# Attention with latent heads and a LoRA layer on one core: the next group's keys and values are projected one to two windows earlier

## The reference

```
q  = rope(x @ w_q);  k = rope(x @ w_k);  v = x @ w_v          # k, v: 8 sets, each used by 4 heads
lk = rope((x @ w_lq) @ w_lk);  lv = x @ w_lv                  # 32 latent heads
out = causal_attn(q, k, v) @ w_o + causal_attn(q, lk, lv) @ w_lo
```

## Time and profile before

| | |
|---|---|
| median of 3 runs | 2101.74 us (2096.83 to 2101.92) |
| the profiled execution's own time | 2100.59 us |
| its span (first to last instruction) | 2098.8 us |
| PE busy | 2037.8 us, 97% |
| DVE, ACT, POOL busy | 1490.7, 1203.1, 893.1 us |
| mean granted PE clock | 0.995 of full speed |

### The profile page before, as it was taken

The page is one execution under the profiler, slowest core; times in us unless marked ns, Lnnn a source line. Parts: engine busy times, 40 slices in busy tenths (PEclk is TensorE's granted clock), DMA queues, the critical chain, the costliest instruction groups (busy, mean ns, idle before and its releaser), DMA issues.

```text
span 2098.8 us, 33401 instructions
## 1 busy us (share of the span) xinstructions
PE 2037.8 (97%) x11724; PEld 1767.5 (84%) x11724; DVE 1490.7 (71%) x2878; ACT 1203.1 (57%) x2503; POOL 893.1 (43%) x687
## 2 busy tenths in 40 slices
PE   6999999999999999999999999999999999999988
PEld 5888888888888888888888888888888888888777
DVE  6677777776776777777777767777677777777765
ACT  3665656666565655566566565666656565556541
POOL 4344444434543454444534444443454345444311
PEclk9999999999999999999999999999999999999999
DMA  3111111111011111211111121111111111111121
GB/s 103 42 38 36 48 28 36 37 42 47 25 44 36 34 42 36 42 31 43 32 43 37 37 48 30 34 37 43 47 26 43 38 32 42 36 43 32 32 51 41
DMA packets 101941, 83.78 MB, mean 40 GB/s; under 512 B 28296, under 2 KB 73992, under 8 KB 101776
## 3 DMA queue, kind: packets, MB, share of 16 engines
q1 hardware_dynamic: 101776, 81.65, 15.8%
HBM read 79.26 MB, written 2.36 MB: 39 GB/s over the span
## 4 chain that ended last, share of the span: by engine, by line
PE 84%; DVE 9%; ACT 3%; issue 3%; DMA 0%; POOL 0%; SPq 0%; ACTq 0%; DVEq 0%
PE scores L502 11%; PE scores L504 11%; PE scores L503 11%; PE bankT L575 10%; PE bankX L502 7%; PE bankX L504 7%; PE bankX L503 7%; PE bankO L502 6%; PE bankO L504 6%; PE bankO L503 6%; DVE rot_half L1087 2%; DVE PT_lo L1077 2%; ACT OT_hi L792 2%; DVE rot_half L1088 1%; ACT rot L792 1%
## 5 line engine op out<-in xcount | busy, mean ns | idle before, releaser
L792 ACT ACTIVATE PT_hi<-bankT 128x512 fp32r<-128x512 f32 (+2 forms) x640 | 336.6, 533 | 353.3 <-PE bankO L504 309.7
L1077 DVE TENSOR_TENSOR PT_lo<-bankT,PT_hi 128x512 fp32r<-128x512 f32 (+2 forms) x640 | 386.8, 608 | 212.4 <-ACT PT_hi L792 210.3
L855 ACT ACTIVATE probs<-probs,nmax 128x128 f32<-128x128 f32 (+7 forms) x512 | 394.6, 772 | 146.0 <-DVE nmax L1071 145.1
L1071 DVE CUSTOM_DVE_ANT_0 probs<-scores,mask 128x128 f32<-128x128 f32 (+7 forms) x512 | 381.4, 750 | 74.6 <-PE scores L504 73.2
L575 PE MATMUL bankT<-ident,probs 128*128 128x128 f32 x2304 | 380.4, 274 | 26.7 <-DVE PT_lo L1077 21.2
L575 PEld LDWEIGHTS bankT<-ident,probs 128*128 128x128 f32 x2304 | 283.9, 141 | 88.3 <-DVE PT_lo L1077 37.3
L1302 POOL TENSOR_TENSOR rot<-rot,cos 128x512 f32<-128x512 f32 x144 | 186.4, 1295 | 201.7 <-DVE rot_half L1088 201.7
L1296 POOL TENSOR_TENSOR OT_lo<-o_raw,OT_hi 128x512 fp32r<-128x512 f32 x64 | 100.1, 1563 | 360.0 <-ACT OT_hi L792 360.0
L792 ACT ACTIVATE OT_hi<-o_raw 128x512 fp32r<-128x512 f32 x128 | 146.7, 1146 | 144.8 <-DVE o_raw L1145 144.8
L1304 POOL TENSOR_TENSOR rot<-rot,rot_half 128x512 f32<-128x512 f32 x144 | 204.2, 1418 | 11.3
L1087 DVE TENSOR_TENSOR rot_half<-rot,sin 64x512 f32<-64x512 f32 x144 | 110.0, 764 | 84.7 <-ACT rot L792 81.1
(11 more groups left out here) (254 smaller groups left out, 5317.0 us busy)
## 6 DMA issues: line engine op xcount, KB each, us to landing
inv_b<-inverses SPq DMA_DIRECT2D x128, 256.0 KB, 3.9
stage<-in_L_attn_w_q SPq DMA_DIRECT2D x32, 256.0 KB, 4.7
stage<-in_L_attn_w_lv SPq DMA_DIRECT2D x32, 256.0 KB, 2.9
stage<-in_L_attn_w_o SPq DMA_DIRECT2D x32, 256.0 KB, 3.8
stage<-in_L_attn_w_lo SPq DMA_DIRECT2D x32, 256.0 KB, 2.6
acc<-in_L_attn_hidden_states SPq DMA_DIRECT2D x8, 256.0 KB, 4.7
stage<-in_L_attn_w_k SPq DMA_DIRECT2D x8, 256.0 KB, 4.9
stage<-in_L_attn_w_v SPq DMA_DIRECT2D x8, 256.0 KB, 5.2
```

What stands on the lines that cost most here:

```text
L792: return act.activation(place, src, ACT.Copy)
L855: act.activation(prob_tile(c, t), prob_tile(c, t), ACT.Exp, bias=nmax[:, c, t:t + 1], scale=-1.0, accum_out=rsum[:, c, t:t + 1]).then_inc( ...
L1071: dve.tensor_tensor_reduce(place, src, tile_view(mask[:, S - width:S], c), -SCALE, -MASKED, ALU.add, ALU.min, nmax[:, c, t:t + 1]).then_in ...
L1077: dve.tensor_tensor(pt_place(1, hh, w, j), bankT[j % 2][:, block_columns(c, j):CH], f32(pt_place(0, hh, w, j)), ALU.subtract).then_inc(pt_ ...
```

## The change

The pieces move within the fourth head of seven groups. K goes to slots 2 and 4 and V of the first half to slot 6 of window 1; V of the second half goes to slot 1 of window 2, VT of the first half to slot 2 of window 2 and VT of the second half to slot 1 of window 3; OUT0 stands in slots 2, 4, 5 and 7 as in the other heads. KT_hi is made by ACT in slots 5 and 7 of window 1. On POOL both K ropes, with their low parts, stand behind Wq's low part in window 1, ahead of the window's OT_lo. Before each VT, PE waits for the copy to vT by its own count.

```diff
         out = {s: ("OUT1", n) for n, s in enumerate((1, 3, 5, 7))}
-        return {**({0: ("LV", 1)} if more else {}), **out}
+        ahead = {2: ("K", 0), 4: ("K", 1), 6: ("V", 0)} if next_group else {}
+        return {**({0: ("LV", 1)} if more else {}), **out, **ahead}
     if w == 2:
-        ahead = {0: ("K", 0), 1: ("K", 1), 2: ("V", 0)} if next_group else {}
+        ahead = {1: ("V", 1), 2: ("VT", 0)} if next_group else {}
         return {**ahead, 3: ("Q", 0)} if more else {}
     ahead = {0: ("Q", 1)} if more else {}
     if next_group:
-        ahead.update({1: ("V", 1), 2: ("VT", 0), 3: ("VT", 1)})
-    slots = (4, 5, 6, 7) if hh == GROUP - 1 else (2, 4, 5, 7)
+        ahead.update({1: ("VT", 1)})
+    slots = (2, 4, 5, 7) if more else (4, 5, 6, 7)
...
                 elif name == "VT":
+                    pe.wait_ge(x_free, n_free(g, hh, *((1, 6), (2, 1))[n]))
                     mm = value_transposes(n, bank)
...
-            highs[GROUP - 1].update({(2, 3): ("K", 0), (3, 0): ("K", 1)})
+            highs[GROUP - 1].update({(1, 5): ("K", 0), (1, 7): ("K", 1)})
...
-                        if w == 3 and s in (2, 3) and more and hh == GROUP - 1:
-                            if s == 2:
-
-                                act.wait_ge(pv_done, last_block(g, hh, 1) + 1 + C_PV)
-                            value_high(n_piece(g, hh, 3, s), V[0], s - 2, piece_bank(g, hh, 3, s))
+                        if name == "VT":
+
+                            act.wait_ge(pv_done, last_block(g, hh, 1) + 1 + C_PV)
+                            value_high(n_piece(g, hh, w, s), V[0], n, piece_bank(g, hh, w, s))
...
-                            if (w, s) in ((0, 3), (2, 3), (3, 1)):
+                            if (w, s) in ((0, 3), (3, 1)) or name == "K":
...
+                    if w == 1 and k_no:
+                        rope_add(*k_no[0], 0)
+                        rope_low(*k_no[0], KT, (ALL, chunk(0)))
+                        rope_add(*k_no[1], 1)
+                        rope_low(*k_no[1], KT, (ALL, chunk(1)))
                     if w == 1:
                         out_low(g, hh, w)
...
                     if w == 2 and more:
-                        k_no = [(rope_no(g, hh, "K", n), rope_no(g, hh, "K", n) % RING) for n in range(2)] if hh == GROUP - 1 else []
-                        if hh == GROUP - 1:
-                            rope_add(*k_no[0], 0)
-                            rope_add(*k_no[1], 1)
-                            rope_low(*k_no[0], KT, (ALL, chunk(0)))
                         rope_add(rope_no(g, hh, "Q", 0), rope_no(g, hh, "Q", 0) % RING, 0)
-                        if hh == GROUP - 1:
-                            rope_low(*k_no[1], KT, (ALL, chunk(1)))
```

More of the change, by code:

```diff
@@ L1349, in group_of_heads @@
                             fetched_low(g, hh, "Wlv0", Wlv0)
+                    k_no = [(rope_no(g, hh, "K", n), rope_no(g, hh, "K", n) % RING) for n in range(2)] \
+                        if more and hh == GROUP - 1 else []
+                    if w == 1 and k_no:
[3 more added lines that the diff above has]
+                        rope_low(*k_no[1], KT, (ALL, chunk(1)))
                     if w == 1:
```

## The result

The changed kernel takes 2124.84 us (2123.72 to 2127.18, 4 runs) against 2101.83 for the kernel before. The ratio is 1.012, with a 95% interval of 1.0106 to 1.0133: slower by 1.2%. The forecast was 2119, with a range of 2100 to 2131; its sign and its mechanism hold, and the size is 5.8 us short. The profiled execution's span is 2121.7 us, 22.9 more than before.

The account below looks back on a forecast made before the run. PE bounds the kernel (2037.8 of 2098.8 us busy), so only its waits count. Windows 1 to 3 grow 2.64 us in each of seven groups, 18.5 us on 2100.59: 2119 us, range 2100 to 2131.

Parts of the forecast that it names:

- The waits that the change removes: Fourth heads, windows 2 and 3: PE waits of 1.00, 1.06 and 0.51 us a group, at most 18.0 us to win.
- Wk's low part: Window 1, first K: PE waits 0.70 us for POOL's Wk_lo, plus 0.1 for the restart.
- the sum: Windows 1 to 3 of a fourth head: 27.14, 17.88 and 18.57, together 63.59 against 60.95; 2.64 us more a group.
- ACT's queue held at the second KT_hi: Window 2's start: PT_hi stands behind that copy, PE waits 2.4 us, the third score tile 0.2 more; chance 0.62.
- The chain: Window 1 into 2: POOL and ACT steps from Wq_hi to the end of o_raw, 11.5 us with handovers.
- The bank between V, the turning and Q: Window 2, bankX: the first turning waits 0.3 us for V's copy, Q 1.4 for the turned values.
- DVE beside POOL: Window 1, turn of K1: a DVE loss has cover, a POOL loss adds up to 1.4 us; taken as 0.
- the rival that gave 2129: Window 1: key's turn and POOL exclude each other at POOL's cost, 1.4 us more in the chain; chance 0.15.
- Window 2: Fourth head's second window: 10.38 + 2.77 + 0.43 + 2.4 + 0.2 + 0.3 + 1.4 = 17.88 us.
- the wait of the third score tile: Window 2: that tile waits 0.4 us for the first row maximum, 0.2 more than in the third head.

Follow-up runs that it names:

- e4: The changed kernel with Wk's low part on POOL ahead of the second latent key's low part: 2125.84 us, ratio 1.012 to the kernel before.
- e5: The changed kernel with the second KT_hi in slot 1 of window 2 and Wk's low part ahead of the second latent key's: 2096.55 us, ratio 0.9978.
- e1: The changed kernel with ACT's second KT_hi in slot 1 of window 2 instead of slot 7 of window 1: 2104.62 us, ratio 1.0018.
- e2: The changed kernel with the first key's cos and add ahead of Wq's low part on POOL: 2106.51 us, ratio 1.0026.
- e3: The changed kernel with both turnings of the values in window 3, slots 1 and 3: 2119.23 us, ratio 1.0087.
- e7: The changed kernel with first key's cos and add ahead of Wq's low part, Wk's low part early, both turnings in window 3: 2088.39 us, ratio 0.9938.
- e8: The kernel before with only the first half's V moved, from slot 2 of window 2 to slot 6 of window 1: 2126.42 us, ratio 1.0125.
- e6: The changed kernel with second KT_hi in slot 1 of window 2, Wk's low part early, both turnings in window 3: 2094.57 us, ratio 0.9972.

## Why the prediction was right, and where its size was off

*The waits that the change removes*: right. With V and the turnings moved, window 3 of the changed kernel is 18.56 against 18.57 forecast.

*Wk's low part*: right. PE's first matmul with Wk waited for POOL (1262.22 + 1.28 = 1263.50; the matmul starts at 1263.65), and e4 and e5 show the price, 0.82 to 0.91 us of window 1 against 0.80 in the sum.

*ACT's queue held at the second KT_hi*: right in place, cause and size. The chain took 11.55 us against 11.5, and the price in window 2 is 2.73 by e1 against 2.6 in the sum. The weight loads stood 1.88 + 0.46 = 2.34 us where the sum has 2.4. That it starts at Wq_hi because of POOL's order is what e2 shows.

*The bank between V, the turning and Q*: right. Both waits together are 1.7 in the sum, and e3 with the clock at full shows 1.66 net of what window 3 takes up.

*DVE beside POOL*: half right. The turn of the second key took 2.1 us more than alone:

```profile
1276.71 1.79 DVE L1088 TENSOR_TENSOR rot_half<-rot,sin 64x512 f32<-64x512 f32 x1
1278.52 1.69 DVE L1089 TENSOR_TENSOR rot_half<-rot,sin 64x512 f32<-64x512 f32 x1
```

Each half ended 0.54 us behind POOL's operation of that time (1278.50 against 1277.96, 1280.21 against 1279.67), as in the earlier trace rows; that is 0.15 less than the 0.69 of a half alone, which the prediction let pass as the same. POOL lost 0.35 once (1.63 against 1.28), not 1.4, so the rival that gave 2129 didn't come. The step said that DVE's loss has cover, since only a row maximum is late. That step was short: the tile's exponential started at 1280.97, and the next weight load for a transpose waited 0.17 us for it (PEld at 1281.84). It is what window 1 has over the forecast, 27.31 against 27.14. In e7, where the turn took 0.69 + 1.68, that wait isn't there, and window 1 is 26.29 against e4's 26.49.

*Window 2* is 18.04 against 17.88; the term that was sized too small is the wait of the third score tile, taken as 0.2. PEld stood 0.68 us there, and in e1, where PT_hi is in time, 0.25: 0.43 of it hangs on ACT's queue.

*The clock* is the term that the sum didn't have. The granted clock fell to half for 3.4 us in window 2 of two groups of the profiled execution. So the 22.9 us of the span divide into 7 x 2.96 = 20.7, about 2.3 for two falls (the lengths are 1.1 to 1.2 more), and small remainders elsewhere. The mean granted clock differs from run to run of one program: the changed kernel's four runs, from the fastest to the slowest, have 0.994, 0.994, 0.993 and 0.992. The order fits, but that the clock makes the 3.5 us between them wasn't tried. The profiled run is the fastest, 1.1 us under the median; so the 5.8 us that the forecast is short are some 2.2 by the windows (7 x 0.32), 2.3 by the two falls and 1.1 that no trace shows.

## What to carry to other kernels

Where engines take their work in order, a moved piece has to be followed through every helper's queue: what stands behind it there is what pays, here PT_hi behind a copy that waited for POOL. Ask of a piece not only what it waits for but what it covers; e8 took one projection away from in front of such a chain and lost 25 us, the slower clock among them. And before making a late helper's reader later (e1), try making its input earlier (e2). Alone, the later reader was the better cure by 1.9 us (2104.62 against 2106.51). With the other two edits it was the worse by 6.2 (e6 against e7), since the late copy held back POOL's queue, and the backlog then met DVE's turn of Q.

## What the runs showed of the hardware

PE's granted clock fell from full to half (2.4 to 1.2 GHz) when PE was back at dense work, behind waits of 1.56 and 0.25 us; the fall lasted 3.41. The three stretches of a window 2 in the changed kernel:

```profile
1029.12:1033.95 4.83, 3.02 (x19) 2.45 (x18) 1.76 (x5) 1.88 (x4) 3.01 (x3) 1.00 0.01 2
1033.95:1037.36 3.41, 3.41 (x10) 2.58 (x9) 2.01 (x6) 3.12 (x7) 1.54 (x1) 0.50 0.08 5
```

And what PE did just before (timeline of PE):

```profile
1032.93 0.44 PE L576 MATMUL bankT<-ident,probs 128*128 128x128 f32 x2 [1.56 <-DVE PT_lo L1078]
1033.62 0.48 PE L503 MATMUL bankO<-PT_hi,LV_lo 128*128 128x512 f32 x1 [0.25 <-DVE o_raw L1146]
1033.92 0.60 PE L504 MATMUL bankO<-PT_lo,LV_hi 128*128 128x512 f32 x1
```

PE was idle for 1.81 of 4.83 us, was back at work at 1032.93, and lost the clock 1.0 us later. The same two waits stood in all seven groups, yet only two lost it; with other timing ahead of it, all seven did (e4), and e3 lost it in six. There it came 0.3 to 2.5 us after PE was back. In e1, e2, e5, e6 and e7, whose windows 2 have 1.27, 1.40, 1.27, 0 and 0.13 us of idle time in the fifth group, it fell in none of the fourth heads. So in this kernel the wait had two prices, its own and about 1.1 to 1.6 us of slower work behind it, and the second came or didn't. It can hide a real gain, as in e4, where 0.82 us in each group came to nothing.
